# A graph network on one core: the gathers of the last edge stage's first four chunks are put at the end of the dense stage before it

## What is computed

```python
h = relu(layernorm(x1))
e = relu(concat([h[src], edge_attr]) @ W1a + b1a) @ W1b + b1b
agg = segment_mean(e, dst)
h2 = concat([h, agg, u])
out = x1 + relu(h2 @ W2a + b2a) @ W2b + b2b
```

## Time and profile before

| | us |
|---|---|
| median of 3 runs | 2356.13 |
| lowest, highest | 2349.71, 2362.62 |
| profiled execution, time | 2355.4 |
| profiled execution, span from first to last instruction | 2353.6 |
| barrier between the last two stages (first instruction of `edge_last`) | 1988.45 |
| TensorE busy, share of the span | 1938.3, 82% |
| VectorE | 1655.7, 70% |
| ScalarE | 1313.0, 56% |
| GpSimd | 1185.3, 50% |

### The profile page before, as it was taken

The page is one execution under the profiler, slowest core; times in us unless marked ns, Lnnn a source line. Parts: engine busy times, 40 slices in busy tenths (PEclk is TensorE's granted clock), DMA queues, the critical chain, the costliest instruction groups (busy, mean ns, idle before and its releaser), DMA issues. The chain is left out here.

```text
span 2353.6 us, 32196 instructions
## 1 busy us (share of the span) xinstructions
PE 1938.3 (82%) x7514; PEld 1101.2 (47%) x7514; DVE 1655.7 (70%) x3528; ACT 1313.0 (56%) x2509; POOL 1185.3 (50%) x919
## 2 busy tenths in 40 slices
PE   0899999987995898985565994699999986699887
PEld 0444444443332444443232332477777765355554
DVE  2899999957896999996234896567777773454543
ACT  0788888842221777774222221678777773465552
POOL 4756656338830433433884000555555552688874
PEclk9999999999997999998877897799999998799999
DMA  4788888744222999997343232999999994443441
GB/s 142 218 255 255 259 253 259 223 135 85 41 47 97 329 357 369 370 362 263 102 126 81 62 96 83 272 310 326 317 324 320 312 311 126 119 115 110 119 119 25
DMA packets 289511, 476.31 MB, mean 202 GB/s; under 512 B 85787, under 2 KB 162472, under 8 KB 289199
## 3 DMA queue, kind: packets, MB, share of 16 engines
q1 hardware_dynamic: 239100, 441.09, 59.2%
q0 software_dynamic: 46400, 33.03, 6.9%
q10 hardware_dynamic: 3824, 0.13, 0.1%
HBM read 272.11 MB, written 202.60 MB: 202 GB/s over the span
## 5 line engine op out<-in xcount | busy, mean ns | idle before, releaser
L487 POOL DMA_INDIRECT first_x<-in_x,first_index x200 | 261.4, 1307 | 176.6 <-ACT first_xn L606 92.2
L1010 POOL TENSOR_TENSOR last_xh<-last_xin,last_hin 125x512 f32<-125x512 f32 x100 | 127.0, 1271 | 232.0 <-DMA last_xin<-in_x 225.8
L801 POOL DMA_INDIRECT second_entry<-node_map,second_si x100 | 129.5, 1295 | 208.5 <-DVE second_src_row L814 173.2
L1083 PE MATMUL last_psH<-last_g,W2a 128*128 128x500 f32 x400 | 189.6, 597 | 25.1 <-DVE last_hid L1045 25.0
L1092 PE MATMUL last_psO<-W2b,last_hid 128*125 128x128 f32 x1600 | 191.6, 273 | 0.0
L1092 PEld LDWEIGHTS last_psO<-W2b,last_hid 128*125 128x125 f32 x1600 | 183.2, 188 | 0.9 <-issue 0.9
L1126 POOL DMA_INDIRECT elast_x<-x_rows,elast_si x100 | 134.6, 1346 | 76.9 <-issue 61.9
L355 ACT ACTIVATE last_xn<-last_x,last_nb,last_rstd 125x128 f32<-125x128 f32 x400 | 164.0, 487 | 0.1
L1134 POOL DMA_INDIRECT out<-elast_o,elast_ends x100 | 128.5, 1285 | 48.9 <-issue 48.9
L585 PE MATMUL first_psW<-first_h,W_in 128*128 128x500 f32 x300 | 152.6, 590 | 0.0
L606 ACT ACTIVATE first_xn<-first_x,first_nb,first_rstd 125x128 f32<-125x128 f32 x300 | 131.0, 491 | 35.3 <-DVE first_nb L533 35.3
(11 more groups left out here) (263 smaller groups left out, 5072.9 us busy)
## 6 DMA issues: line engine op xcount, KB each, us to landing
hT<-first_h SPq DMA_DIRECT2D x100, 250.0 KB, 3.2
yT<-first_y SPq DMA_DIRECT2D x100, 250.0 KB, 3.4
second_yin<-yT SPq DMA_DIRECT2D x50, 500.0 KB
second_hin<-hT SPq DMA_DIRECT2D x50, 500.0 KB
yT<-second_y SPq DMA_DIRECT2D x50, 500.0 KB
last_yin<-yT SPq DMA_DIRECT2D x50, 500.0 KB
first_x<-in_x SPq DMA_DIRECT2D x100, 224.0 KB
h_rows<-second_rows SPq DMA_DIRECT2D x50, 448.0 KB
```

What stands on the lines that cost most here:

```text
L487: pool.indirect_dma_start(x[:, to % X, j], None, a["x"], bass.IndirectOffsetOnAxis(index[:, end, r % 2, j:j + 1], 0), bounds_check=NODES - ...
L801: pool.indirect_dma_start(entry[:, q], None, scratch.node_map, bass.IndirectOffsetOnAxis(si[:, q], 0), bounds_check=NODES - 1, oob_is_err= ...
L1083: last = pe.matmul(psH[h][:, 0:CH], w.W2a[:, 0, h * 128:(h + 1) * 128], g[:, q % 2], start=True, stop=True)
```

## The change

Index and row buffers of the first four chunks (`ahead.si`, `ahead.x`) are allocated around both stages and take the place of the ring buffers `si` and `x` of `edge_last`, along with their semaphores. In `dense_last` SP loads four chunks of indices at steps 20 to 23 of its pairs, and after its last output store waits for the edge rows' stores and loads the destination rows of chunks 0 to 3 (8 DMAs), and only then waits for the other stores. GpSimd, behind its last bias sum, waits for all stores to the table and issues the 16 gathers of chunks 0 to 3. In `edge_last` the `load` of SP and the `fetch` of GpSimd do nothing for those chunks; the semaphores' values go on as before, so chunk 4 waits for their second round.

```diff
--- before.py
+++ after.py
@@ -32,6 +32,7 @@
 BIG = 1.0e37
 MAPW = 16
 NOWHERE = 1 << 20
+AHEAD_CHUNKS = 4
 AHEAD = 20
 MAP0 = 12
 
@@ -882,7 +883,7 @@
                 unrolled(NCHUNK, U, [(2, skip), (2, turn), (5, edges(turn_edges))])
 
 
-def dense_last(nc, a, w, scratch, out):
+def dense_last(nc, a, w, scratch, out, ahead):
 
 
 
@@ -961,9 +962,15 @@
                     hold(sp, ph.seen, e.rows, made(c))
                     move_rows(sp, rows_of(scratch.x1, NODES + (ECHUNK - 1) * CH - c * CH), flat(erows, s), e_stored[s])
 
-                unrolled(NCHUNK // 2, U // 2, [(0, load), (2, edges(load_edges, 2)), (4, store_x1), (6, edges(store_edges, 2)), (9, store_o)])
+                def load_ahead(t, q, r):
+                    if t < AHEAD_CHUNKS:
+                        sp.dma_start(ahead.si[:, t], index_slot(scratch.src_row, t * CH)).then_inc(ahead.idx_loaded[t], 16)
+
+                unrolled(NCHUNK // 2, U // 2, [(0, load), (2, edges(load_edges, 2)), (4, store_x1), (6, edges(store_edges, 2)), (9, store_o), (20, load_ahead)])
                 for s in range(2):
                     sp.wait_ge(e_stored[s], 16 + 32 * len(range(s, ECHUNK, 2)))
+                for k in range(AHEAD_CHUNKS):
+                    move_rows(sp, ahead.x[:, k, 0:TILES].rearrange("p j f -> p (j f)"), rows_of(scratch.x1, NODES + k * CH), ahead.x_loaded[k])
                 for q in range(U // 2):
                     for sems in (x1_stored, x1_stored2, o_stored, o_stored2):
                         sp.wait_ge(sems[q], 16 + 16 * len(range(q, NCHUNK // 2, U // 2)))
@@ -1015,6 +1022,15 @@
                     pool.tensor_tensor(x1b[:, q], x1[:, q], w.b2b[:].rearrange("p (o f) -> p o f", o=1).to_broadcast([TILE, TILES, D]), ALU.add).then_inc(m.x1b, 1)
 
                 unrolled(NCHUNK, U, [(0, add_h2), (5, add_bias)])
+
+                for s in range(2):
+                    pool.wait_ge(e_stored[s], 16 + 32 * len(range(s, ECHUNK, 2)))
+                for q in range(U // 2):
+                    for sems in (x1_stored, x1_stored2):
+                        pool.wait_ge(sems[q], 16 + 16 * len(range(q, NCHUNK // 2, U // 2)))
+                for k in range(AHEAD_CHUNKS):
+                    pool.wait_ge(ahead.idx_loaded[k], 16)
+                    gather(pool, ph.seen, ahead.x[:, k, TILES:2 * TILES], scratch.x1, ahead.si[:, k], ahead.moved[k])
 
             @block.vector
             def _(dve):
@@ -1496,13 +1512,13 @@
                 steps(C, [(0, weigh), (0, total), (1, combine)])
 
 
-def edge_last(nc, a, w, scratch, out):
+def edge_last(nc, a, w, scratch, out, ahead):
 
     U = 4
     N2 = 2 * TILES
-    with phase(nc, "elast") as ph:
-        si, ends = (ph.sb(n, [TILE, U, TILES], I32) for n in ("si", "ends"))
-        x = ph.sb("x", [TILE, U, N2, D])
+    with phase(nc, "elast", ahead.idx_loaded + ahead.x_loaded + ahead.moved) as ph:
+        si, x, idx_loaded, x_loaded, moved = ahead.si, ahead.x, ahead.idx_loaded, ahead.x_loaded, ahead.moved
+        ends = ph.sb("ends", [TILE, U, TILES], I32)
         xb = ph.sb("xb", [TILE, U, TILES, D])
         ea = ph.sb("ea", [TILE, U, TILES, D])
         xn = ph.sb("xn", [TILE, 2, N2, D])
@@ -1520,9 +1536,7 @@
         psH = [ph.ps(f"psH{s}") for s in range(2)]
         psG = [ph.ps(f"psG{s}") for s in range(2)]
         psM, psO = ph.ps("psM"), ph.ps("psO")
-        idx_loaded, ends_loaded, x_loaded, ea_loaded, run_loaded = (
-            ph.loaded(n, U) for n in ("idx_loaded", "ends_loaded", "x_loaded", "ea_loaded", "run_loaded"))
-        moved, placed = ph.loaded("moved", U), ph.loaded("placed", U)
+        ends_loaded, ea_loaded, run_loaded, placed = (ph.loaded(n, U) for n in ("ends_loaded", "ea_loaded", "run_loaded", "placed"))
         names = ("xb stats sd rstd nb xn xT g eaT eT hid0 hid1 hidden psm msg tot mean "
                  "hidden2 hid20 hid21 o_ps o init")
         m = Group(**{n: ph.stage(n + "_made") for n in names.split()})
@@ -1533,6 +1547,8 @@
                 ph.start(sp)
 
                 def load(k, q, r):
+                    if k < AHEAD_CHUNKS:
+                        return
                     hold(sp, ph.seen, m.stats, made(k - U))
                     sp.dma_start(si[:, q], index_slot(scratch.src_row, k * CH)).then_inc(idx_loaded[q], 16)
                     hold(sp, ph.seen, m.xb, made(k - U))
@@ -1761,8 +1779,13 @@
             dense_second(nc, a, w, scratch, edge)
             attention(nc, a, w, scratch, 1, edge)
         batch_norm_params(nc, w, 1)
-        dense_last(nc, a, w, scratch, out)
-        edge_last(nc, a, w, scratch, out)
+        with ExitStack() as both:
+            outer = lambda n, s, d=F32: both.enter_context(nc.sbuf_tensor("ahead_" + n, s, d))
+            sems = lambda n: [nc.alloc_semaphore(f"ahead_{n}{q}") for q in range(AHEAD_CHUNKS)]
+            ahead = Group(si=outer("si", [TILE, AHEAD_CHUNKS, TILES], I32), x=outer("x", [TILE, AHEAD_CHUNKS, 2 * TILES, D]),
+                          idx_loaded=sems("idx_loaded"), x_loaded=sems("x_loaded"), moved=sems("moved"))
+            dense_last(nc, a, w, scratch, out, ahead)
+            edge_last(nc, a, w, scratch, out, ahead)
 
 
 # ---- launch ----
```

## The result

Twenty runs of each, medians: **2347.23 us against 2355.78**. One of the twenty runs of the changed kernel took 9898 us and is left out of the ratio as disturbed. The ratio is 0.9956, 95% interval 0.9935 to 0.9976. That is 10.4 us less (5.7 to 15.3 by the interval), where 16.4 were forecast. The 0.44% lies just inside the bound of 0.5% that the prediction called no change. The profiled execution has a span of 2339.4 and a time of 2341.14.

A forecast was written before the change was run, and what follows sets the result against it. The last edge stage's middle goes at GpSimd's pace, so its run's start counts: 17.5 us for the head less 1.1 for SP's issues is 16.4, from 2355.4 to 2339.0, plus 0.7 for the median: 2339.7 us, range 2331 to 2348.

The forecast's parts named there:

- part 1: End of dense stage: 16 gathers before the barrier take 25.1 us, not held, GpSimd done 0.9 us before SP.
- part 2: SP at the dense stage's end: eight row loads take 3.5 us and make the barrier 1.1 us later.
- The bound beside it: SP's output waits: 1 MB of loads at some 250 GB/s could delay one 4 us, only if overtaking the store.
- part 3: Head of the last edge stage: without the wait for gathers, chunk 0 is normalised 16.4 us earlier.
- part 4: Edge stage from chunk 4: normally no loss, at worst 4 us; chunk 7's gather and GpSimd's run move 16.4 us earlier.
- Rival 1: Edge stage head: TensorE's clock drops less often, saving 3 us more, 2336.5; chance 0.10.
- Rival 2: Edge stage: chunk 4 becomes the late one, up to 4 us return before VectorE's fifth statistics, 2343; chance 0.12.
- Rival 5: Nothing arrives: the start of GpSimd's unbroken run in the edge stage does not move, 2355; chance 0.04.
- Rival 3: Gathers before the barrier are held by VectorE, barrier 9.1 us beyond the forecast, up to 2348.8; chance 0.07.
- Rival 4: GpSimd starts its early gathers late, after the output stores: 7.6 us slower, 2363.7, or 2374.7 with held gathers; chance 0.05.
- the term that took everything in front of the barrier for unchanged: Dense stage: chunk index loads go between SP's issues, which wait for data, costing 0, at most 1.1 us.

The follow-up runs named there:

- experiment 2: The kernel before, run again unchanged for a second profile: ratio 1.0009 (0.9987 to 1.003).
- experiment 9: The kernel before plus the buffers around the dense stage (never filled with rows) and the four index loads: 1.7 +- 4.7 us above the kernel before.
- experiment 1: The changed kernel, run again unchanged: 2343.95 us against 2354.59 for the kernel before, ratio 0.9963.
- experiment 10: The changed kernel with its four index loads behind the dense stage's last data load: 11.5 +- 4.5 us under the kernel before.
- experiment 7: The changed kernel with all 25 chunks' indices in one load during the dense stage: 22.7 +- 5.2 us under the kernel before, ratio 0.9899.
- experiment 3: The changed kernel with the eight destination-row loads back behind the barrier, only gathers ahead: 12.5 +- 4.9 us under the kernel before.
- experiment 11: The changed kernel with row loads between the last output stores and all indices in one load behind the last data load: 2324.59 us, ratio 0.986.
- experiment 5: The changed kernel with GpSimd also waiting for the output stores before its 16 gathers: 14.1 +- 6.4 us above the kernel before.
- experiment 4: The changed kernel with the 16 gathers back behind the barrier, only plain row loads ahead: 7.2 +- 3.9 us above the kernel before.
- experiment 12: The changed kernel's full dense stage with the old edge stage, which fetches everything again: 11.7 +- 5.4 us above the kernel before.
- experiment 6: The changed kernel with the eight row loads issued between the dense stage's last output stores: 16.0 +- 4.5 us under the kernel before.

## Why the prediction came out as it did

The range held the time. The change is faster, but not by the 0.5% that was given 0.75 (0.44%, interval 0.24 to 0.65), and the gain was 6 us smaller.

**Gathers in front of the barrier (part 1): right.** 24.9 us, not held, done before SP.

**SP's loads (part 2): undersized.** 1.1 us was forecast; 2.3, 1.8 and 2.2 were measured in three profiles. The eight loads take 3.9 us instead of 3.5, the first of them 0.95 to issue instead of 0.31, and SP's wait for the other engines at the end of the block is 1.1 us instead of 0.2. The bound beside it took some 250 GB/s for the head's rate; from 1990 to 2005 it was 208 in the kernel before. The sum did not use it.

**The head (part 3): right in its mechanism, 1.5 us too large.** Taken from the last output sum, chunk 0 is normalised at 26.6, 26.9 and 27.6 us in three profiles with the old edge stage head (before, experiments 2 and 9) and at 12.3, 11.8 and 12.2 in three with the change (after, experiments 1 and 10): 14.9 us. I had 16.4. The rest is SP's loads and the counters that SP raises (1.2 us), which the gathers' wait had hidden.

**Chunk 4 and on (part 4): right.** Chunk 4's first gather came at 2001.93, a little after the 1998 to 2001 given, since its indices took 6.5 us to land and not 2.5 to 5; VectorE did not wait for its rows. Chunk 7's gather came 15.9 us earlier on the same count (67.5 to 51.6).

**The rivals.** Rival 1 (the clock) is real, but for single executions: the clock fell in the pause before chunk 1's hidden layer in 12 of the 14 profiles, not in experiments 2 and 7. The 32 us that begin 72 before the end had a granted clock of 0.89 or 0.95 in ten of them and 1.00 in experiments 1, 3, 7 and 11. Rivals 2 and 5 did not happen, 3 not in the dense stage, and 4 only where experiment 5 made it.

The whole last stretch took 370.9, 373.1 and 375.2 us, and 357.8, 353.4 and 356.0 with the change: **17.3 us less, in three profiles against three**. Of these, 15.9 are there at chunk 7's gather; the rest is within the 302 to 307 us that what follows takes anyway. So the forecast's mechanism and its size are borne out in the part that it was about. The times give 9 to 12.

**What the sum had wrong is the term that took everything in front of the barrier for unchanged** (of the index loads: "0, at most 1.1 us"). The dense stage took 476.8, 477.5 and 476.0 us in the three profiles without the change, and 480.3, 491.2 and 486.6 with it. In all nine profiles with four index loads and early fetches of any kind it was 477.0 to 491.2, mean 481.9. In the profiles, that is where the missing us lie.

Why is open, and so is whether the change does it.

- Not the place of the index loads, and not these loads and the buffers by themselves (experiments 9, 10). The early fetches come after the part that got longer.
- Not the larger set of semaphores by itself: experiments 7 and 11 allocate the same twelve and fetch early too, and have 476.4 and 474.9.
- What remains is a mixture of these, or chance in a stage whose DMA engines are full: twenty runs of the kernel before alone reach from 2347.78 to 2375.67.
- Experiments 4 and 12 speak for a real cost: their times are 9 us above what their last stretches explain. Experiments 6 and 11 speak against it: their times are all that the last stretches promise, or more.

The time lies 0.8 us inside the upper end of the range, 2348. With a miss of 6 us in the gain, that it holds is in part luck.

## What to carry to other kernels

When a stage starts by waiting for indirect DMAs, issue the first ones under the drain of the stage before, where their engine is idle; the gain is the hole at the head, and it reaches the end only if the unbroken run of the pacing engine starts earlier by as much. Then look at what stands between that engine and its next work. Here it was small index loads, which SP issued only after a wait for an earlier chunk and behind larger loads. Taking them ahead gave some 10 us more in the last stretch (up to 3 of it may be the clock's) and 12 in the times, with intervals of 5 to either side. Which of the two, the wait or the place behind larger loads, cost more was not tried. And weigh a gain of half a per cent against what the other stages do by themselves: cut profiles at a fixed event and compare the parts, several profiles of each kernel, before crediting or blaming the change.

## What was not expected of the hardware

An indirect DMA's issue on GpSimd that starts while VectorE runs an instruction with two SBUF inputs waits for its end. In the middle of the kernel before there are 18 long issues (1.78 to 2.15 us instead of 1.25), one for each chunk. All had begun during the running total or the mean, and all ended 0.98 to 1.06 us after it. With one input in PSUM all but one were gone, and that one had begun during the bias sum. An issue that started before such an instruction was not lengthened (29 in the kernel before, 1.19 to 1.29 us). The Trainium skill, "SBUF — State Buffer", section "Who interferes with whom", says that such an instruction contends with a GpSimd instruction that reads SBUF; the trace agrees (1.92 against 1.27). The prediction had seen one such row and asked only whether it would happen at the new place; in the middle of the stage it is 14 us. TensorE's clock after the same pause of 3.3 us was at its higher level (1.00, 2.4 GHz, 1.11 us a pair) in two profiles and at its lower (0.50, 1.2 GHz, 2.04 us) in twelve: up to 3 us of scatter from the head of one stage alone.
